# Expert stage of a macaron block: 71 instead of 72 token tiles per call, with one tile in the last pair

## The chip, the cores and the metric

The program runs on one core of one Trainium2 chip. Its engines work side by side, each through its own instruction list, and meet only at semaphores: TensorE (PE, with its weight loads listed apart as PEld), VectorE (DVE), ScalarE (ACT), GpSimd (POOL) and SyncE (SP), which only issues DMA transfers here. The metric is the device time of one execution in microseconds (us); the comparison takes the median of several executions. Smaller is better.

## The reference: what is computed

The input `x` is 4 sequences of 1024 tokens with 128 features, so 4096 tokens. Three layers follow each other:

```
x = x + 0.5 * ffn(layernorm(x))        # call 0 of the expert layer
x = x + mixer(layernorm(x))            # a state-space mixer and its own feed-forward part
x = x + 0.5 * ffn(layernorm(x))        # call 1 of the expert layer, same weights
```

and `ffn` has a shared part and a routed part:

```
shared = (silu(x @ sw1) * (x @ sw2)) @ sw3
w, idx = top_k(softmax(x @ rw + rb), 2)            # 2 of 8 experts for each token
routed = sum over the 2 experts e: w_e * ((silu(x @ ew1[e]) * (x @ ew2[e])) @ ew3[e])
```

Each token meets two of eight experts, so there are 8192 pairs of a token and an expert in each call.

## The kernel before

**Sorting.** For each call POOL scatters 8192 rows of normalised tokens into a DRAM buffer `xs` (L710, 128 rows each). Every expert has a region of its own there. A tile is 128 consecutive rows of one region. The number of tiles that an expert fills is its count divided by 128, rounded up, and DVE works out on the chip where each tile lies (`row_at`) and whose it is (`tile_e`). The program has a fixed number of tiles, `NT = 2 * TOK // P + NE` = 72 for a call. Tiles beyond the filled ones are read from a dummy region, whose rows carry a destination that is out of bounds. The filled tiles can be at most 71: the 8192 rows fill 64 tiles, and rounding up for 8 experts adds less than 8 in all, in whole tiles. How many are filled depends on the data.

**Expert loop.** The tiles go in `NPAIR` = 36 pairs, numbered p. For a pair the work is, in this order:

- SP loads both tiles from `xs` into a ring of 8 slots (L462); `tile_in` counts the landings of each slot.
- PE transposes them (`pe_tiles_t`, L2025), ACT rounds the result to the upper part `xt_hi` (L1018), DVE takes the rest `xt_lo` (L1506) and the destinations `dest` of the rows (L1511).
- PE multiplies with the up weights of the tile's expert, three matmuls of 512 columns for a tile (`pe_up_e`, L2038 to L2040).
- ACT takes the silu (L1026) and DVE the product `hid` (L1521).
- PE transposes `hid` (`pe_hid_t`, L2051, two for a tile), ACT copies it out (L1035), PE multiplies with the down weights (`pe_down_e`, L2064, two for a tile, each of which the trace records as two).
- DVE copies the answer out of PSUM to `y_out`, a ring of 4 slots of two tiles (`dve_answer`, L1531).
- POOL scatters it to the DRAM buffer `ys` with one indirect DMA for each tile (`pool_answers`, L726); `y_stored` counts the landings of each slot. Rows whose destination is out of bounds are skipped.

The order is written out by hand. In step p PE does the up matmuls of pair p + 1, the transposes of `hid` of pair p, the down matmuls of pair p - 1 and the tile transposes of pair p + 3. In the names of the trace, `ps_a` and `ps_b` hold the up products of even and odd pairs, `ps_go` and `ps_tr` the transposes and answers in turn, and `arena` is the memory in which `x_tiles`, `y_out` and the copied `hid` lie.

**End of a call.** SP waits until all four `y_stored` semaphores have their full count (L464), then loads the answers back from `ys` (L469) in blocks of 512 tokens. In call 0 DVE adds them to `x` (L1539), and the mixer starts from that; in call 1 ACT and DVE add them (L1042, L1551, L1555) and SP stores the result (L472).

```
                for r in range(YRING):
                    sp.wait_ge(y_stored[r], 32 * (NPAIR // YRING) * (call + 1))
```

Of the kernel before, what the change touches and what calls it, by code (L numbers as in the profile page):

```python
# [5 lines left out]
F32 = mybir.dt.float32  # L6
# [5 lines left out]
ACT = mybir.ActivationFunctionType  # L12

P = 128
# [74 lines left out]
def macaron(nc, A, out):  # L89
    ctx = ExitStack()  # L90
    with ctx:
# [36 lines left out]
        y_out = part(0, [P, YRING, 2, P])  # L128
# [63 lines left out]

        ps_turn = (ps_k, ps_t, ps_r)

        def ps_tiles(p):
            return ps_turn[(2 * p + 1) % 3][:, 0:2 * P]

        def ps_answers(p):
            return ps_turn[(2 * p + 2) % 3][:, 0:2 * P]

# [209 lines left out]
        def _(sp):  # L410
# [33 lines left out]
            for call in range(2):  # L444

                sp.wait_ge(pads_ready, call + 1)
                pads = table(mybir.EngineType.SP, pad_row, 0, NE, DUMMY - P)
                for e in range(NE):
                    sp.dma_start(xs[bass.ds(pads[e], P), :], fill[:, :]).then_inc(pads_stored, 16)
                sp.wait_ge(tiles_ready, call + 1)  # L450
                at = list(table(mybir.EngineType.SP, row_at, 0, GROUP, DUMMY))
                sp.wait_ge(pads_stored, 16 * NE * (call + 1))
                sp.wait_ge(scattered, 16 * 2 * TOK // P * (call + 1))

                sp.wait_ge(b_ps_ready, 2 * NB * (call + 1))
                for i in range(NT):
                    if i and i % GROUP == 0:
                        at += list(table(mybir.EngineType.SP, row_at, i, min(GROUP, NT - i), DUMMY))
                    if i >= XIN:
                        sp.wait_ge(t_ps_ready, call * NPAIR + (i - XIN) // 2 + 1)  # L460
                        sp.wait_ge(dest_ready, call * NPAIR + (i - XIN) // 2 + 1)
                    sp.dma_start(x_tiles[:, i % XIN, :], xs[bass.ds(at[i], P), :]).then_inc(tile_in[i % XIN], 16)  # L462
                for r in range(YRING):
                    sp.wait_ge(y_stored[r], 32 * (NPAIR // YRING) * (call + 1))  # L464
                ring = BACK[call]
                for n in range(NB):
                    if n >= ring:
                        sp.wait_ge(combined, call * NB + n - ring + 1)
                    sp.dma_start(y_in[call][:, n % ring, :, :], yv[n]).then_inc(block_in[n], 16)  # L469
# [542 lines left out]
        def act_split(act, call, p):  # L1012

            pair = call * NPAIR + p
            act.wait_ge(t_ps_ready, pair + 1)
            if pair >= 2:
                act.wait_ge(up_e_ps_ready, pair - 1)
            act.activation(xt_hi[:, p % 2, :], ps_tiles(p), ACT.Copy).then_inc(hi_ready, 1)  # L1018

        def act_silu_e(act, call, p):  # L1020

            pair = call * NPAIR + p
            act.wait_ge(up_e_ps_ready, pair + 1)
            if pair >= 2:
                act.wait_ge(hid_e_done, pair - 1)
            act.activation(silu_a[:, p % 2, :].rearrange("p (j h) -> p j h", j=2), ps_pair[p % 2][:, :, 0:HID],  # L1026
                           ACT.Silu).then_inc(silu_e_done, 1)

        def act_hid_t(act, call, p):

# [4 lines left out]
            act.activation(hid_t[:, p % 2, :], ps_d, ACT.Copy).then_inc(ht_ready, 1)  # L1035

        def act_finish(act):
            for n in range(NB):
# [463 lines left out]
        def dve_split(dve, call, p):  # L1502

            pair = call * NPAIR + p
            dve.wait_ge(hi_ready, pair + 1)
            dve.tensor_tensor(xt_lo[:, p % 2, :], ps_tiles(p), xt_hi[:, p % 2, :].bitcast(F32),  # L1506
                              ALU.subtract).then_inc(lo_ready, 1)
            for j in range(2):
                i = 2 * p + j
                dve.wait_ge(tile_in[i % XIN], 16 * ((call * NT + i) // XIN + 1))  # L1510
                r = dve.scalar_tensor_tensor(dest[:, i:i + 1], x_tiles[:, i % XIN, P:P + 1], tile_e[:, i:i + 1],  # L1511
                                             x_tiles[:, i % XIN, P + 1:P + 2], ALU.not_equal, ALU.add)
            r.then_inc(dest_ready, 1)

        def dve_hid_e(dve, call, p):

            pair = call * NPAIR + p
            dve.wait_ge(silu_e_done, pair + 1)
            if pair >= 2:
                dve.wait_ge(ht_ps_ready, pair - 1)  # L1520
            dve.tensor_tensor(hid[:, p % 2, 0, :].rearrange("p (j h) -> p j h", j=2),  # L1521
                              silu_a[:, p % 2, :].rearrange("p (j h) -> p j h", j=2), ps_pair[p % 2][:, :, HID:],
                              ALU.mult).then_inc(hid_e_done, 1)

        def dve_answer(dve, call, p):

            pair = call * NPAIR + p
            dve.wait_ge(y_ps_ready, pair + 1)
            if p >= YRING:
                dve.wait_ge(y_stored[p % YRING], 32 * (call * (NPAIR // YRING) + p // YRING))  # L1530
            dve.tensor_copy(y_out[:, p % YRING, :, :], ps_answers(p).rearrange("p (j d) -> p j d", j=2)).then_inc(answer_ready, 1)  # L1531

        def dve_combine(dve, own, call, n):

# [481 lines left out]
        def pe_tiles_t(pe, call, p):  # L2016

            pair = call * NPAIR + p

            if p >= 5:  # L2020
                pe.wait_ge(answer_ready, pair - 4)
            for j in range(2):
                i = 2 * p + j
                pe.wait_ge(tile_in[i % XIN], 16 * ((call * NT + i) // XIN + 1))
                r = pe.transpose(ps_tiles(p)[:, j * P:(j + 1) * P], x_tiles[:, i % XIN, 0:P], ident[:, :])  # L2025
            r.then_inc(t_ps_ready, 1)

        def pe_up_e(pe, call, p, which):

            pair = call * NPAIR + p  # L2030
            pe.wait_ge(lo_ready, pair + 1)
            after(pe, hid_e_done, pair - 1)
            for j in range(2):
                hi = up_hi[:, bass.ds(which[2 * p + j], 1), :].rearrange("p a h -> p (a h)")
                lo = up_lo[:, bass.ds(which[2 * p + j], 1), :].rearrange("p a h -> p (a h)")
                target = ps_pair[p % 2][:, j, :]
                mine = slice(j * P, (j + 1) * P)
                pe.matmul(target, xt_hi[:, p % 2, mine], hi, start=True, stop=False)  # L2038
                pe.matmul(target, xt_hi[:, p % 2, mine], lo, start=False, stop=False)  # L2039
                r = pe.matmul(target, xt_lo[:, p % 2, mine], hi, start=False, stop=True)  # L2040
            r.then_inc(up_e_ps_ready, 1)

        def pe_hid_t(pe, call, p):

            pair = call * NPAIR + p
            pe.wait_ge(hid_e_done, pair + 1)
            after(pe, ht_ready, pair)
            for j in range(2):
                for k in range(2):
                    at = (2 * j + k) * P  # L2050
                    r = pe.transpose(ps_d[:, at:at + P], hid[:, p % 2, 0, at:at + P], ident[:, :])  # L2051
            r.then_inc(ht_ps_ready, 1)

        def pe_down_e(pe, call, p, which):
# [3 lines left out]

            if p + 2 >= NPAIR:
                pe.wait_ge(answer_ready, pair - 2)  # L2060
            for j in range(2):
                for k in range(2):
                    at = (2 * j + k) * P
                    r = pe.matmul(ps_answers(p)[:, j * P:(j + 1) * P], hid_t[:, p % 2, at:at + P],  # L2064
                                  w_down_e[:, bass.ds(which[2 * p + j], 1), k, :].rearrange("p a d -> p (a d)"),
                                  start=(k == 0), stop=(k == 1))
            r.then_inc(y_ps_ready, 1)

# [139 lines left out]
```

## Time and profile before

| | us |
|---|---|
| median of 3 runs | 791.8 (791.72 to 792.77) |
| the profiled execution, its own time | 793.16 |
| span of its trace | 791.1 |
| expert loop of call 0, first to last scatter of answers | 120.9 to 223.9 |
| expert loop of call 1, last scatter of answers | 767.9 |
| PE busy in the span | 649.5 (82%) |
| POOL busy in the span | 519.5 (66%) |

The page gives busy shares of the engines for the whole span, which has five stages: shared feed-forward and routing (0 to 104 us), the experts of call 0 (to 226), the mixer (to about 600, with the routing of call 1 begun inside), the shared part of call 1 (to 652) and the experts of call 1 with the final sum. A share of busy time says little about any one of them. The chain of work that ended last is the view that tells for each stretch which engine set the pace, and the timeline shows the instructions around one place. Idle time is written in square brackets, with what ended it; "issue" there means that the engine waited for nothing that the profile shows.

### The profile page before, as it was taken

What the parts mean: (1) busy time and instruction counts of PE and PEld (TensorE: products, weight loads), DVE (VectorE), ACT (ScalarE), POOL (GpSimd) and SP (SyncE); (2) the same over time, 40 slices, a digit from 0 to 9 for tenths busy, and PEclk for the clock granted to TensorE, in tenths of its full rate; (3) what the DMA queues carried; (4) which work ended last, traced back from release to release, by engine and by line L of the source; (5) the groups of instructions that cost most, each with busy time, mean ns of one, the idle gap of its engine ahead of it and who ended that gap; (6) DMA issues with size and microseconds to landing.
All of it is one profiled execution on the core that took longest, in us unless ns stands there. A gap on an engine that the chain in (4) does not pass through costs nothing.

```text
span 791.1 us, 13711 instructions
## 1 busy us (share of the span) xinstructions
PE 649.5 (82%) x3768; PEld 478.4 (60%) x3768; DVE 548.8 (69%) x1706; ACT 424.9 (54%) x745; POOL 519.5 (66%) x656
## 2 busy tenths in 40 slices
PE   3478979999907298989999997999978979999950
PEld 2245558888802155657576665667635557889840
DVE  5666756656549669897999999899735635566637
ACT  1122224554407999898999998643213214445525
POOL 3777765666646676887898869676754442666660
PEclk9988989999957588999999999979989998999995
DMA  9511223333142000000000000000010113333218
GB/s 264 161 45 51 78 69 85 88 88 92 57 143 77 0 1 1 0 2 1 1 2 1 1 15 15 14 15 22 21 34 25 58 35 87 86 94 89 79 30 316
DMA packets 49368, 46.34 MB, mean 59 GB/s; under 512 B 8456, under 2 KB 42861, under 8 KB 49296
## 3 DMA queue, kind: packets, MB, share of 16 engines
q1 hardware_dynamic: 40592, 28.54, 12.9%
q0 software_dynamic: 8704, 16.93, 6.6%
q8 instruction: 34, 0.56, 0.3%
q14 instruction: 38, 0.31, 0.2%
HBM read 25.30 MB, written 21.19 MB: 59 GB/s over the span
## 4 chain that ended last, share of the span: by engine, by line
PE 30%; POOL 25%; issue 16%; DVE 12%; DMA 8%; ACT 8%; POOLq 1%; SPq 0%; DVEq 0%; ACTq 0%
POOL xs L710 11%; POOL ys L726 11%; DMA xs<-rows,pos 6%; PE ps_tr L1662 4%; PE ps_go L1662 3%; PE ps_tr L2064 2%; PE ps_go L2051 1%; PE ps_go L1833 1%; PE ps_tr L1850 1%; PE ps_go L1837 1%; PE ps_b L1884 1%; POOL rstd L700 1%; PE ps_go L1883 1%; PE ps_a L2038 1%; PE ps_a L2039 1%
## 5 line engine op out<-in xcount | busy, mean ns | idle before, releaser
L726 POOL DMA_INDIRECT ys<-arena,dest x144 | 140.8, 978 | 88.9 <-issue 64.7
L710 POOL DMA_INDIRECT xs<-rows,pos x128 | 127.0, 993 | 76.2 <-DMA xs<-rows,pos 32.3
L1006 ACT ACTIVATE silu_a<-ps_a 128x512 f32<-128x512 f32 x32 | 19.1, 597 | 62.0 <-PE ps_a L2002 62.0
L2064 PE MATMUL ps_tr<-w_down_e,arena 128*128 x384 | 50.7, 275 | 0.0
L1521 DVE TENSOR_TENSOR hid<-silu_a,ps_a 128x512 f32<-128x512 f32 x36 | 24.8, 688 | 34.8 <-ACT silu_a L1026 34.8
L1521 DVE TENSOR_TENSOR hid<-silu_a,ps_b 128x512 f32<-128x512 f32 x36 | 24.8, 688 | 34.3 <-ACT silu_a L1026 34.3
L2064 PEld LDWEIGHTS ps_tr<-w_down_e,arena 128*128 128x128 f32 x384 | 46.7, 192 | 0.0
L1035 ACT ACTIVATE arena<-ps_go 128x512 f32<-128x512 f32 x72 | 42.6, 592 | 2.0 <-PE ps_go L2051 2.0
L1488 DVE TENSOR_TENSOR hid<-silu_a,ps_b 128x512 f32<-128x512 f32 x32 | 21.9, 687 | 31.2 <-PE ps_b L2004 29.3
L2051 PE MATMUL ps_go<-ident,hid 128*128 128x128 f32 x288 | 43.2, 272 | 0.2
L1026 ACT ACTIVATE silu_a<-ps_a 128x512 f32<-128x512 f32 x36 | 21.5, 597 | 38.4 <-PE ps_a L2040 38.4
L1026 ACT ACTIVATE silu_a<-ps_b 128x512 f32<-128x512 f32 x36 | 21.5, 597 | 37.9 <-PE ps_b L2040 37.9
L2051 PEld LDWEIGHTS ps_go<-ident,hid 128*128 128x128 f32 x288 | 35.5, 140 | 10.1 <-DVE hid L1521 0.8
L1018 ACT ACTIVATE xt_hi<-ps_tr 128x256 fp32r<-128x256 f32 x48 | 18.5, 385 | 40.2 <-PE ps_tr L2025 40.2
L1833 PE MATMUL ps_go<-arena,state 128*128 128x128 f32 x128 | 31.7, 332 | 7.8 <-DVE us L1291 6.9
L2012 PEld LDWEIGHTS ps_go<-w_shared_down,hid 128*128 128x128 f32 x256 | 31.2, 194 | 7.7 <-issue 7.7
L1833 PEld LDWEIGHTS ps_go<-arena,state 128*128 128x128 f32 x128 | 21.8, 204 | 19.7 <-issue 13.9
L1963 PE MATMUL ps_tr<-ident,rows 128*128 128x128 f32 x64 | 13.3, 343 | 24.5 <-DVE rows L1404 19.8
L2012 PE MATMUL ps_go<-w_shared_down,hid 128*128 128x128 f32 x256 | 31.5, 276 | 1.7 <-DVE x L1493 1.7
L2038 PE MATMUL ps_a<-up_hi,xt_hi 128*128 x72 | 32.3, 449 | 0.0
L1662 PE MATMUL ps_go<-arena,w_tap 128*128 128x512 f32 x64 | 32.1, 647 | 0.0
L2038 PE MATMUL ps_b<-up_hi,xt_hi 128*128 x72 | 31.8, 441 | 0.0
(368 smaller groups left out, 2042.3 us busy)
## 6 DMA issues: line engine op xcount, KB each, us to landing
arena<-xs SPq DMA_DIRECT2D x144, 65.0 KB, 1.9
rows<-ys SPq DMA_DIRECT2D x8, 512.0 KB, 3.8
arena<-ys SPq DMA_DIRECT2D x8, 512.0 KB, 7.1
ys<-arena,dest POOLq DMA_INDIRECT x144
x<-in_L_attn_x SPq DMA_DIRECT2D x8, 256.0 KB, 4.5
arena<-in_L_ffn_ew SPq DMA_DIRECT2D x4, 512.0 KB, 7.0
xs<-rows,pos POOLq DMA_INDIRECT x128
out<-x SPq DMA_DIRECT2D x8, 256.0 KB, 4.8
```

Source lines behind the costliest of these rows:

```text
L710: pool.indirect_dma_start(xs, bass.IndirectOffsetOnAxis(pos[:, n, i:i + 1], 0), rows[:, n * TT + i % TT, :], None).then_inc(scattered, 16)
L726: pool.indirect_dma_start(ys, bass.IndirectOffsetOnAxis(dest[:, i:i + 1], 0), y_out[:, p % YRING, j, :], None, bounds_check=2 * TOK - 1, o ...
L1026: act.activation(silu_a[:, p % 2, :].rearrange("p (j h) -> p j h", j=2), ps_pair[p % 2][:, :, 0:HID], ACT.Silu).then_inc(silu_e_done, 1)
L1035: act.activation(hid_t[:, p % 2, :], ps_d, ACT.Copy).then_inc(ht_ready, 1)
L1488: dve.tensor_tensor(hid[:, turn % 2, k, :], silu_a[:, k, :], ps_b[:, k, :], ALU.mult).then_inc(hid_done, 1)
L1521: dve.tensor_tensor(hid[:, p % 2, 0, :].rearrange("p (j h) -> p j h", j=2), silu_a[:, p % 2, :].rearrange("p (j h) -> p j h", j=2), ps_pai ...
L1662: r = pe.matmul(target, weights(k), zt[:, shift:shift + BT], start=(k == 0), stop=(k == taps - 1))
L1833: pe.matmul(pb["o"][:, at], state[:, k % 2, p * P:(p + 1) * P], cfs[:, q, k * P:(k + 1) * P], start=True, stop=False)
L2012: r = pe.matmul(ps_d[:, t * P:(t + 1) * P], hid[:, turn % 2, k, t * P:(t + 1) * P], w_shared_down[:, k, :], start=(k == 0), stop=(k == 1))
L2038: pe.matmul(target, xt_hi[:, p % 2, mine], hi, start=True, stop=False)
L2051: r = pe.transpose(ps_d[:, at:at + P], hid[:, p % 2, 0, at:at + P], ident[:, :])
L2064: r = pe.matmul(ps_answers(p)[:, j * P:(j + 1) * P], hid_t[:, p % 2, at:at + P], w_down_e[:, bass.ds(which[2 * p + j], 1), k, :].rearrange ...
```

## The change

The program has `LIVE = NT - 1` = 71 tiles in a call. Pairs 0 to 34 are as they were; pair 35 has one tile. Two helpers say which tiles a pair has and how many landings a ring slot gets in a call:

```diff
+LIVE = NT - 1
+def tiles_of(p):
+    return range(2 * p, min(2 * p + 2, LIVE))
+def in_ring(r, ring, of=1):
+    return sum(i // of % ring == r for i in range(LIVE))
...
-                for i in range(NT):
+                for i in range(LIVE):
...
-                    sp.wait_ge(y_stored[r], 32 * (NPAIR // YRING) * (call + 1))
+                    sp.wait_ge(y_stored[r], 16 * in_ring(r, YRING, 2) * (call + 1))
...
-            for j in range(2):
-                i = 2 * p + j
+            for j, i in enumerate(tiles_of(p)):
                 pool.indirect_dma_start(ys, bass.IndirectOffsetOnAxis(dest[:, i:i + 1], 0),
...
-            act.activation(silu_a[:, p % 2, :].rearrange("p (j h) -> p j h", j=2), ps_pair[p % 2][:, :, 0:HID],
+            act.activation(halves(silu_a[:, p % 2, :], p), ps_pair[p % 2][:, 0:len(tiles_of(p)), 0:HID],
                            ACT.Silu).then_inc(silu_e_done, 1)
...
-            for j in range(2):
-                i = 2 * p + j
-                pe.wait_ge(tile_in[i % XIN], 16 * ((call * NT + i) // XIN + 1))
+            for j, i in enumerate(tiles_of(p)):
+                pe.wait_ge(tile_in[i % XIN], 16 * (call * in_ring(i % XIN, XIN) + i // XIN + 1))
                 r = pe.transpose(ps_tiles(p)[:, j * P:(j + 1) * P], x_tiles[:, i % XIN, 0:P], ident[:, :])
```

The other functions of the loop take the same form: their operand is half as wide for pair 35, and of full width for all others. Slot 7 of the tile ring gets 8 landings in a call and the others 9; slot 3 of the answer ring gets 17 and the others 18.

On PE, at the end of the loop of call 0, this stood before, from the up matmuls of pair 35 (`ps_b`) to the transposes of its `hid`. The first rows are those of its second tile, which come straight behind the three matmuls of its first:

```order
L2038 ISA
L2038 MATMUL ps_b<-up_hi,xt_hi 128x512
L2039 REGISTER_ALU
L2039 MATMUL ps_b<-up_lo,xt_hi 128x512
L2040 MATMUL ps_b<-up_hi,xt_lo 128x512
L2051 MATMUL ps_go<-ident,hid 128x128 x4
L2064 ISA
L2064 MATMUL ps_tr<-w_down_e,arena 128x128
```

and now this stands there, from the matmuls of the first tile on (the lines are numbered 13 higher in the changed kernel here):

```order
L2051 ISA
L2051 MATMUL ps_b<-up_hi,xt_hi 128x512
L2052 REGISTER_ALU
L2052 MATMUL ps_b<-up_lo,xt_hi 128x512
L2053 MATMUL ps_b<-up_hi,xt_lo 128x512
L2064 MATMUL ps_go<-ident,hid 128x128 x4
L2077 ISA
L2077 MATMUL ps_tr<-w_down_e,arena 128x128
```

The block of five rows stands once ahead of the transposes of pair 34 instead of twice, and all that follows on PE moves up by it: the transposes of pair 34, the down matmuls of pair 33, and so on.

On POOL, between the constants of the mixer and its first norm, the scatters of the answers of call 0 stood before in one group of 72 (line 726),

```order
L501 AFFINE_SELECT own_head<-own_head 128x256
L726 DMA ys<-arena,dest 8192x128 x72
L528 TENSOR_SCALAR asmall<-amv 128x4
L529 TENSOR_TENSOR arstd<-asmall,minus_half 128x4
L530 TENSOR_TENSOR asmall<-arstd 128x4
```

and now in one of 71:

```order
L516 AFFINE_SELECT own_head<-own_head 128x256
L740 DMA ys<-arena,dest 8192x128 x71
L543 TENSOR_SCALAR asmall<-amv 128x4
L544 TENSOR_TENSOR arstd<-asmall,minus_half 128x4
L545 TENSOR_TENSOR asmall<-arstd 128x4
```

One scatter is gone at the end of the group, and nothing changes place. The second call has the same two differences, and SP has one load of `xs` fewer in each call.

## Rows read from the trace of the kernel before

**Rows 1.** The page: span, PE and POOL busy, chain by engine.
```profile
span 791.1 us, 13711 instructions
PE 649.5 (82%) x3768; PEld 478.4 (60%) x3768; DVE 548.8 (69%) x1706; ACT 424.9 (54%) x745; POOL 519.5 (66%) x656
...
PE 30%; POOL 25%; issue 16%; DVE 12%; DMA 8%; ACT 8%; POOLq 1%; SPq 0%; DVEq 0%; ACTq 0%
```

**Rows 2.** Timeline of the steady loop: start us, length us, engine, line, operation.
```profile
119.27 0.25 PEld L2025 LDWEIGHTS ps_go<-ident,arena 128*128 128x128 f32 x2
...
122.21 0.25 PEld L2025 LDWEIGHTS ps_tr<-ident,arena 128*128 128x128 f32 x2
...
122.52 0.42 DVE L1531 COPY arena<-ps_tr 128x256 f32<-128x256 f32 x1
...
123.78 0.97 POOL L726 DMA_INDIRECT ys<-arena,dest  x1 [0.54 <-issue]
```

**Rows 3.** Timeline, end of call 0, PE's weight loads and DVE.
```profile
210.28 0.26 PEld L2025 LDWEIGHTS ps_tr<-ident,arena 128*128 128x128 f32 x2
...
210.50 0.19 PEld L2038 LDWEIGHTS ps_a<-up_hi,xt_hi 128*128 128x128 f32 x1
...
213.53 0.42 DVE L1531 COPY arena<-ps_go 128x256 f32<-128x256 f32 x1
...
213.79 0.19 PEld L2038 LDWEIGHTS ps_b<-up_hi,xt_hi 128*128 128x128 f32 x1
...
214.49 0.59 PEld L2051 LDWEIGHTS ps_go<-ident,hid 128*128 128x128 f32 x4
...
216.25 0.42 DVE L1531 COPY arena<-ps_tr 128x256 f32<-128x256 f32 x1
...
218.91 0.42 DVE L1531 COPY arena<-ps_go 128x256 f32<-128x256 f32 x1 [0.61 <-PE ps_go L2064]
```

**Rows 4.** Timeline, end of call 0, POOL's scatters of answers.
```profile
214.79 0.97 POOL L726 DMA_INDIRECT ys<-arena,dest  x1 [0.68 <-issue]
...
217.51 0.97 POOL L726 DMA_INDIRECT ys<-arena,dest  x1 [0.47 <-issue]
...
218.78 0.97 POOL L726 DMA_INDIRECT ys<-arena,dest  x1 [0.30 <-issue]
...
222.61 0.97 POOL L726 DMA_INDIRECT ys<-arena,dest  x1 [0.30 <-issue]
223.89 0.97 POOL L726 DMA_INDIRECT ys<-arena,dest  x1 [0.30 <-issue]
```

**Rows 5.** Chain of work, end of call 0: start us, length us, what.
```profile
223.89 2.10 DMA ys<-arena,dest
...
226.07 3.85 DMA rows<-ys
```

**Rows 6.** DMA from 218 to 226 us: forty slices of 0.2 us, GB/s.
```profile
GB/s 0 0 0 0 0 328 0 0 0 0 0 50 2 0 0 0 0 0 3 0 0 0 0 0 2 1 0 0 0 0 0 3 0 0 0 0 0 3 0 0
```

**Rows 7.** All scatters of answers: shortest, median and longest duration in ns.
```profile
L726 POOL DMA_INDIRECT ys<-arena,dest x144: 969/980/1092, 120.9 to 767.9; - x144
```

**Rows 8.** Timeline, end of call 1, the same engines.
```profile
754.28 0.26 PEld L2025 LDWEIGHTS ps_tr<-ident,arena 128*128 128x128 f32 x2
...
758.79 0.98 POOL L726 DMA_INDIRECT ys<-arena,dest  x1 [0.66 <-issue]
...
762.79 0.98 POOL L726 DMA_INDIRECT ys<-arena,dest  x1 [0.31 <-issue]
...
767.95 0.98 POOL L726 DMA_INDIRECT ys<-arena,dest  x1 [0.30 <-issue]
```

**Rows 9.** Chain of work, end of call 1.
```profile
767.95 2.11 DMA ys<-arena,dest
```

**Rows 10.** Busy us by stretch: PE, PEld, DVE, ACT, POOL, then granted clock, DMA share.
```profile
340.00:350.00 10.00, 9.73 (x37) 5.46 (x36) 8.89 (x16) 9.88 (x15) 9.66 (x11) 0.83 0.01 2
235.00:240.00 5.00, 0.00 (x0) 0.00 (x0) 4.86 (x23) 1.24 (x4) 4.26 (x11) 0.50 0.38 120
```

More of the change, by code:

```diff
@@ L1017, in act_split @@
                 act.wait_ge(up_e_ps_ready, pair - 1)
-            act.activation(xt_hi[:, p % 2, :], ps_tiles(p), ACT.Copy).then_inc(hi_ready, 1)
+            act.activation(xt_hi[:, p % 2, 0:len(tiles_of(p)) * P], ps_tiles(p), ACT.Copy).then_inc(hi_ready, 1)
         def act_silu_e(act, call, p):
@@ L1034, in act_hid_t @@
                 act.wait_ge(y_ps_ready, pair - 1)
-            act.activation(hid_t[:, p % 2, :], ps_d, ACT.Copy).then_inc(ht_ready, 1)
+            width = len(tiles_of(p)) * HID
+            act.activation(hid_t[:, p % 2, 0:width], ps_d[:, 0:width], ACT.Copy).then_inc(ht_ready, 1)
         def act_finish(act):
@@ L1505, in dve_split @@
             dve.wait_ge(hi_ready, pair + 1)
-            dve.tensor_tensor(xt_lo[:, p % 2, :], ps_tiles(p), xt_hi[:, p % 2, :].bitcast(F32),
+            mine = slice(0, len(tiles_of(p)) * P)
+            dve.tensor_tensor(xt_lo[:, p % 2, mine], ps_tiles(p), xt_hi[:, p % 2, mine].bitcast(F32),
                               ALU.subtract).then_inc(lo_ready, 1)
-            for j in range(2):
-                i = 2 * p + j
-                dve.wait_ge(tile_in[i % XIN], 16 * ((call * NT + i) // XIN + 1))
+            for i in tiles_of(p):
+                dve.wait_ge(tile_in[i % XIN], 16 * (call * in_ring(i % XIN, XIN) + i // XIN + 1))
                 r = dve.scalar_tensor_tensor(dest[:, i:i + 1], x_tiles[:, i % XIN, P:P + 1], tile_e[:, i:i + 1],
@@ L1529, in dve_answer @@
             if p >= YRING:
[L1530 to L1531 removed]
+                dve.wait_ge(y_stored[p % YRING], 16 * (call * in_ring(p % YRING, YRING, 2) + 2 * (p // YRING)))
+            dve.tensor_copy(y_out[:, p % YRING, 0:len(tiles_of(p)), :], ps_answers(p).rearrange("p (j d) -> p j d", d=P)).then_inc(answer_ready, 1)
         def dve_combine(dve, own, call, n):
@@ L2032, in pe_up_e @@
             after(pe, hid_e_done, pair - 1)
-            for j in range(2):
-                hi = up_hi[:, bass.ds(which[2 * p + j], 1), :].rearrange("p a h -> p (a h)")
-                lo = up_lo[:, bass.ds(which[2 * p + j], 1), :].rearrange("p a h -> p (a h)")
+            for j, i in enumerate(tiles_of(p)):
+                hi = up_hi[:, bass.ds(which[i], 1), :].rearrange("p a h -> p (a h)")
+                lo = up_lo[:, bass.ds(which[i], 1), :].rearrange("p a h -> p (a h)")
                 target = ps_pair[p % 2][:, j, :]
@@ L2047, in pe_hid_t @@
             after(pe, ht_ready, pair)
-            for j in range(2):
+            for j in range(len(tiles_of(p))):
                 for k in range(2):
@@ L2060, in pe_down_e @@
                 pe.wait_ge(answer_ready, pair - 2)
-            for j in range(2):
+            for j, i in enumerate(tiles_of(p)):
                 for k in range(2):
@@ L2064, in pe_down_e @@
                     r = pe.matmul(ps_answers(p)[:, j * P:(j + 1) * P], hid_t[:, p % 2, at:at + P],
-                                  w_down_e[:, bass.ds(which[2 * p + j], 1), k, :].rearrange("p a d -> p (a d)"),
+                                  w_down_e[:, bass.ds(which[i], 1), k, :].rearrange("p a d -> p (a d)"),
                                   start=(k == 0), stop=(k == 1))
```

11 lines of the change are left out of this document (5 added, 6 removed).

## The prediction

> **What bounds the kernel now.** I read the page first, then the chain of work that ended last, then the timeline at the two places where a call of the experts ends. The page shows no engine that is the bound for the whole span: PE is busy 82% and POOL 66% of it, and the chain gives PE 30% and POOL 25% [rows 1]. So the question is what sets the pace where the removed tile stood, and the tile stood at the very end of each call.
>
> In the steady loop the tile transposes of two neighbouring pairs start at 119.27 and 122.21 us, a period of 2.94 us, and PE has no gap in it. POOL follows: the answer copy starts at 122.52 and the scatter at 123.78, 1.26 us later [rows 2]. Two scatters behind each other take POOL 1.28 us each (below), 2.56 us for a pair, less than 2.94. POOL has room there and PE paces.
>
> At the end this turns round. PE has no more up matmuls to do, and the answer copies come at 213.53, 216.25 and 218.91 us, the last being that of pair 35 [rows 3]. POOL is still issuing: its last scatters start at 218.78, two more in between, then 222.61 and 223.89 [rows 4], (223.89 - 218.78) / 4 = 1.28 us apart. The answer of pair 35 lay ready for over 3 us before its scatter began. What ends the call is the last scatter: the chain goes from its start at 223.89 through 2.10 us of landing to the load of the answers at 226.07 [rows 5], and nothing else runs. Call 1 ends in the same way: 762.79 and 767.95 with three scatters between them, 1.29 us apart [rows 8], and a landing of 2.11 us [rows 9]. Everything behind these two points waits for the loaded answers, the mixer in one case and the final sum in the other.
>
> **What the last scatter carries.** After the peak of 328 GB/s and a remainder of 50 GB/s the DMA moves 3 GB/s or less in any slice [rows 6]. The issues behind it belong to tiles without rows. They cost the same as others: shortest, median and longest scatter are 969, 980 and 1092 ns [rows 7], and the 2.10 us of landing in rows 5 is that of an empty one. So an empty tile is not cheap, and taking it away is worth a whole issue.
>
> **The change part by part.** First the scatter. One issue fewer stands at the end of each queue of POOL: 1.28 us in call 0 and 1.29 us in call 1, all on the path [rows 4, 8].
>
> Second, POOL's unbroken run starts earlier. It begins with the first scatter of pair 32 at 214.79 [rows 4], 1.26 us behind the answer copy of 213.53 [rows 3], so it is tied to PE. Ahead of that answer the change removes one of the two transposes of pair 35's tiles. The two take from 210.28 to 210.50 [rows 3], so one is 0.11 us. In call 1 the same pair of loads stands at 754.28 [rows 8]. The run starts 0.11 us earlier in each.
>
> Third, a small wait inside the run goes. The scatter of pair 33 starts at 217.51, which is 2.72 us and not 2 x 1.28 = 2.56 us behind 214.79 [rows 4], because its answer copy of 216.25 was late [rows 3]. In the new order three up matmuls of pair 35 are missing ahead of the down matmuls of pair 33. They take from 213.79 to 214.49 [rows 3], 0.70 us. With the transpose the answer is ready 0.81 us earlier if PE paces it, at 215.44, and its scatter could start at 216.70. POOL is free for it at 214.68 + 2.56 = 217.24. So POOL paces from there, with 0.5 us to spare, and the 0.16 us are gained. DVE does the product of pair 35 ahead of this copy; it is half as wide and its silu starts earlier too, so it does not hold the copy up.
>
> The sum for call 0: seven scatters stand from pair 32 on, with six steps between them, so the last starts at 214.68 + 6 x 1.28 = 222.36 in place of 223.89, a gain of 1.53 us. For call 1: 758.79 - 0.11 + 6 x 1.29 = 766.42 in place of 767.95 [rows 8], again 1.53 us. Together 3.06 us.
>
> The rest costs and gives nothing. The other down matmuls and transposes of pair 35, its shorter copies on ACT and DVE and one load on SP all lie before the answer copy of 218.91, over 3 us ahead of need. If that cover were gone, the 0.5 us above would be the first to be felt. The first 35 pairs have operands of the same shape, the semaphores have other constants, and no wait is added. SP waits for the same four semaphores, and the fullest still comes last. PE's list is shorter by nine rows in each call. What this does to the fetching of instructions no row shows; I bound it by -0.3 and +0.3 us, the size of POOL's ordinary gap between scatters [rows 4], and take zero.
>
> Against the profiled execution this makes the span 791.1 - 3.06 = 788.0 us. Its own time, 793.16, lies 1.4 us above the median of 791.8. A shift in two places applies to each run alike, so I take it off the median: 791.8 - 3.1 = 788.7 us.
>
> **A rule against it.** Each scatter keeps POOL for 1.28 us though its data are nil [rows 4, 6]. The Trainium skill, "DMA: Bandwidth & Descriptors", section "Anatomy of one DMA — SWDGE (gpsimd) path", says that nearly all of the fixed 2 us of such a transfer is the receipt of the write at its end, and that making the descriptors is small. By that rule issues would overlap with landings and one issue fewer would be worth near nothing, which is the time of rival (a). The landing of 2.10 us agrees [rows 5]; the steps between issues do not, and the sum goes by the steps.
>
> **Rivals.** (a) The end is not set by the last issue but by the last scatter with data. Then the empty issue was free, and only the earlier start counts: 0.11 + 0.16 = 0.27 us a call, 791.3 us. For it speaks that all data had gone by 220.4 us, 1.6 us behind the issue of 218.78 [rows 4, 6]. Against it speaks the chain, in which the load of the answers follows the landing of the issue at 223.89 by 0.08 us [rows 5], as it must if each semaphore counts every scatter.
>
> (b) The gain of call 0 is given back in the mixer, through TensorE's clock. The clock is at half, 1.2 GHz, when the mixer begins (0.50 at 235 to 240 us, PE idle before), and inside it there are drops such as 340 to 350 us with a granted mean of 0.83 while PE is busy 9.73 of 10 us [rows 10]. That mean is (1 - 0.83) / 0.5 = a third of the stretch, 3.4 us, at half speed, and at worst half of that, 1.7 us, is lost. All that follows stands 1.5 us earlier, and a drop may come in or go. One more makes 788.7 + 1.7 = 790.4 us, within 0.2% of before; one fewer makes 787.0. The Trainium skill, "TensorE: Matmul & The Clock Gate", section "Part 1: The HAM clock gate", says that the gate watches activity on a count that runs free of the kernel, so that the same program ramps at different places from run to run. By that, such drops would be spread over runs of both kernels alike, and the sum would stay. The three runs of before lie within 1.05 us of each other.
>
> (c) Slower: the same mechanism several times. Two more drops (3.4 us) eat the gain and decide the sign, and three make 788.7 + 5.1 = 793.8 us. For it: the mixer keeps PE, ACT and POOL all over 9 us of 10 busy in rows 10, so that lost PE time has little slack. Against it: nothing inside the mixer changes its order, and PE is idle for as long as before ahead of it, since its own end and the load of the answers both move up by about 1.5 us.
>
> (d) The change doesn't take the issue away because the list of POOL is the same. The order shows 71 in place of 72, so I give this no chance.
>
> **How the numbers follow.** Forecast, the whole 3.1 us: 0.80, with a spread of about 0.9 us from the bounds and from medians of three runs. One more drop of the clock: 0.08. One fewer: 0.04. Empty scatter free (a): 0.05. Slower (c): 0.03. What a measurement can tell from no change is 0.2%, 1.6 us. Faster by more than that are the forecast and one drop fewer, 0.84. Within it lie (a) and one more drop, 0.13. Slower is 0.03. The range reaches from 787.4 to 790.3 us: it holds the forecast's own spread and most of the case with one more drop, and leaves out 787.0 and (a).
>
> **What would show it.** After the change POOL's list of answers should have 142 scatters. In call 0 the run of steps of 1.28 us should begin with the first scatter of pair 32, 0.1 us earlier than 214.79, with no step of 1.45 us in it, and the last should start at 222.4; in call 1 the load of the answers should follow the last scatter by 2.2 us as now, and the rest, 21 us, should keep its length. The mixer's stretch should be as long as before: from the load of the answers of call 0 to the last scatter of call 1, 767.95 - 226.07 = 541.9 us, it should be 1.5 us shorter, 540.4. I am wrong if the last scatter starts less than 1 us earlier, which would mean that PE or a landing paces the end, or if that stretch grows, which would be the clock.

## The result and the profile after

| | before | changed kernel |
|---|---|---|
| median of 8 runs each, us | 792.52 (791.64 to 793.4) | 789.51 (788.24 to 791.18) |
| ratio, 95% interval | 1 | 0.9963 (0.9949 to 0.9976) |
| span of the trace, us | 791.1 | 789.0 |

The kernel became 3.0 us faster where 3.1 was forecast; the interval of the ratio reaches from 1.9 to 4.0 us. The page of the changed kernel is nearly that of before [rows 1]: two scatters fewer, shares the same.

```profile
span 789.0 us, 13649 instructions
PE 643.9 (82%) x3748; PEld 473.3 (60%) x3748; DVE 545.4 (69%) x1704; ACT 423.9 (54%) x745; POOL 519.5 (66%) x654
...
PE 46%; POOL 15%; DVE 12%; issue 10%; DMA 8%; ACT 8%; SPq 0%; POOLq 0%; DVEq 0%; ACTq 0%
```

The last line, the chain by engine, gives PE 46% and POOL 15%, where it was 30% and 25%. That is no change of the loop. The chain is followed back from the end: in the kernel before it stays with POOL through the last pairs, and in the changed kernel it leaves POOL at the scatter of 217.92, goes to a copy of DVE, and follows PE from there. The shares of a chain can jump like this where two engines run at one pace.

The timeline of the end of call 0 shows the unbroken run that was forecast, as [rows 3, 4] did for the kernel before (columns: start us, length us, engine, line, operation).

```profile
210.97 0.14 PEld L2038 LDWEIGHTS ps_tr<-ident,arena 128*128 128x128 f32 x1
...
214.10 0.42 DVE L1545 COPY arena<-ps_go 128x256 f32<-128x256 f32 x1
...
215.36 0.97 POOL L740 DMA_INDIRECT ys<-arena,dest  x1 [0.57 <-issue]
...
216.14 0.42 DVE L1545 COPY arena<-ps_tr 128x256 f32<-128x256 f32 x1 [0.49 <-PE ps_tr L2077]
...
216.64 0.97 POOL L740 DMA_INDIRECT ys<-arena,dest  x1 [0.30 <-DVE arena L1545]
...
217.92 0.97 POOL L740 DMA_INDIRECT ys<-arena,dest  x1 [0.30 <-DVE arena L1545]
219.20 0.97 POOL L740 DMA_INDIRECT ys<-arena,dest  x1 [0.30 <-issue]
...
223.03 0.97 POOL L740 DMA_INDIRECT ys<-arena,dest  x1 [0.30 <-issue]
```

One tile is transposed where it was two. The answer copy of pair 32 starts at 214.10, its first scatter 1.26 us later, and from there seven scatters stand 1.28 us apart up to 223.03, with no longer step among them. The two small gains can be read one by one. From the last tile transpose to this answer copy it is 214.10 - 210.97 = 3.13 us where it was 213.53 - 210.28 = 3.25 [rows 3]. From the first scatter of pair 32 to that of pair 33 it is 217.92 - 215.36 = 2.56 us where it was 2.72 [rows 4]. The chain of this stretch again goes from the last scatter through its landing to the load of the answers:

```profile
223.03 2.09 DMA ys<-arena,dest
...
225.21 3.73 DMA rows<-ys
```

All scatters of answers together (count, shortest, median and longest duration in ns, first and last start):

```profile
L740 POOL DMA_INDIRECT ys<-arena,dest x142: 970/982/1092, 121.6 to 765.8; - x142
```

The gain is best read from the length of POOL's queue, from the first to the last scatter of a call, since what happens ahead of the loop shifts both ends:

| | call 0 | call 1 |
|---|---|---|
| before | 120.87 to 223.89, 103.02 | 664.86 to 767.95, 103.09 |
| changed | 121.56 to 223.03, 101.47 | 664.24 to 765.79, 101.55 |
| shorter by | 1.55 | 1.54 |

That is 3.09 us, and 3.06 were forecast. The two spans differ by only 2.1 us because in these two executions the first scatter of the changed kernel came 0.69 us later and the stretch between the calls took 0.24 us more (441.21 against 440.97), both outside of the two loops. The prediction named one more length as a sign, from the load of the answers of call 0 to the last scatter of call 1. It is 765.79 - 225.21 = 540.6 us, against 541.9 before and 540.4 forecast.

### The profile page after: what moved, and what is told of

It reads as the page before. It is cut to its first block, busy times and chain, and to the rows that moved or that the text cites. A ratio compares the mean times of both kernels' runs of the same rounds, so it can differ in the third digit from the quotient of the medians.

```text
span 789.0 us, 13649 instructions
## 1 busy us (share of the span) xinstructions
PE 643.9 (82%) x3748; PEld 473.3 (60%) x3748; DVE 545.4 (69%) x1704; ACT 423.9 (54%) x745; POOL 519.5 (66%) x654
## 4 chain that ended last, share of the span: by engine, by line
PE 46%; POOL 15%; DVE 12%; issue 10%; DMA 8%; ACT 8%; SPq 0%; POOLq 0%; DVEq 0%; ACTq 0%
POOL xs L725 11%; DMA xs<-rows,pos 6%; PE ps_tr L2077 5%; PE ps_go L2064 4%; PE ps_tr L1676 4%; PE ps_go L1676 3%; PE ps_go L2077 2%; PE ps_a L2051 2%; PE ps_a L2053 2%; PE ps_a L2052 2%; PE ps_b L2053 2%; PE ps_b L2051 2%; PE ps_b L2052 2%; PE ps_go L1847 1%; PE ps_tr L1864 1%
## 5 line engine op out<-in xcount | busy, mean ns | idle before, releaser
L740 POOL DMA_INDIRECT ys<-arena,dest x142 | 139.1, 980 | 88.3 <-issue 62.4
L1536 DVE TENSOR_TENSOR hid<-silu_a,ps_a 128x512 f32<-128x512 f32 x36 | 24.8, 688 | 35.7 <-ACT silu_a L1040 35.7
L1536 DVE TENSOR_TENSOR hid<-silu_a,ps_b 128x512 f32<-128x512 f32 (+1 forms) x36 | 24.2, 673 | 32.9 <-ACT silu_a L1040 31.6
L1503 DVE TENSOR_TENSOR hid<-silu_a,ps_b 128x512 f32<-128x512 f32 x32 | 21.9, 686 | 30.9 <-PE ps_b L2018 29.0
L1040 ACT ACTIVATE silu_a<-ps_b 128x512 f32<-128x512 f32 (+1 forms) x36 | 21.1, 585 | 37.0 <-PE ps_b L2053 37.0
L1032 ACT ACTIVATE xt_hi<-ps_tr 128x256 fp32r<-128x256 f32 (+1 forms) x48 | 18.3, 380 | 41.5 <-PE ps_tr L2038 41.5
L1522 DVE TENSOR_TENSOR xt_lo<-ps_tr,xt_hi 128x256 fp32r<-128x256 f32 (+1 forms) x48 | 20.1, 419 | 16.7 <-ACT xt_hi L1032 16.4
```

The costliest lines, as they stand in the source:

```text
L1040: act.activation(halves(silu_a[:, p % 2, :], p), ps_pair[p % 2][:, 0:len(tiles_of(p)), 0:HID], ACT.Silu).then_inc(silu_e_done, 1)
L1536: dve.tensor_tensor(halves(hid[:, p % 2, 0, :], p), halves(silu_a[:, p % 2, :], p), ps_pair[p % 2][:, 0:len(tiles_of(p)), HID:], ALU.mult) ...
```

## The experiments

The runs were made in three groups, each with its own runs of the kernel before on its chip. "Length" is from first to last scatter of a call.

### Only the scatter is left out

The kernel before, with the 72nd scatter of each call not issued:

```diff
+                if i == NT - 1:
+                    continue
                 pool.indirect_dma_start(ys, bass.IndirectOffsetOnAxis(dest[:, i:i + 1], 0),
```

(and 17 for 18 scatters in the counts of ring slot 3).

> The kernel before, without the scatter of tile 71 and with nothing else changed: PE, ACT and DVE still do the whole pair 35. The tile holds no rows with these inputs. Theory (POOL's issues pace the end of a call, an empty one costs as much as a full one): the stretch from the first to the last scatter of answers, 103.02 us in call 0 and 103.09 in call 1 of the kernel before, gets 1.28 us shorter in each call, to 101.74 and 101.80, and the time falls by 2.6 us, a ratio of 0.9968. The end of the queue keeps its step of 1.44 us ahead of the scatter of pair 33. Rival (the end is set by the last scatter with data, an empty issue is free): the load of the answers starts as long behind the scatter of tile 67 as before, ratio 1.000.

Measured: ratio 0.9980 (0.9966 to 0.9995). Lengths 101.74 and 101.80 us, 1.28 and 1.29 below before. The end of its timeline has the old step ahead of pair 33's scatter, 217.77 - 216.32 = 1.45 us, and then steps of 1.28:

```profile
215.04 0.97 POOL L728 DMA_INDIRECT ys<-arena,dest  x1 [0.69 <-issue]
216.32 0.97 POOL L728 DMA_INDIRECT ys<-arena,dest  x1 [0.30 <-issue]
217.77 0.97 POOL L728 DMA_INDIRECT ys<-arena,dest  x1 [0.47 <-issue]
219.04 0.97 POOL L728 DMA_INDIRECT ys<-arena,dest  x1 [0.30 <-issue]
...
222.87 0.97 POOL L728 DMA_INDIRECT ys<-arena,dest  x1 [0.30 <-issue]
225.03 1.28 SPq L469 DMA_DIRECT2D rows<-ys  x3
```

An empty issue costs its whole step. The rival by which only scatters with rows count falls; the load of the answers comes 2.16 us behind the last issue here, and 2.18 in the kernel before.

### Half a pair on PE, all 72 scatters

The changed kernel, with a scatter to out-of-bounds places (`nowhere`) at the end of each call:

```diff
+            if p == NPAIR - 1:
+                pool.wait_ge(route_const, ROUTE_CONST)
+                pool.indirect_dma_start(ys, bass.IndirectOffsetOnAxis(nowhere[:, 0:1], 0),
+                                        y_out[:, p % YRING, 1, :], None, bounds_check=2 * TOK - 1,
+                                        oob_is_err=False).then_inc(y_stored[p % YRING], 16)
```

> The changed kernel, with a 72nd scatter of answers put back at the end of each call, all of whose destinations are out of bounds. PE, ACT and DVE do one tile in pair 35. Theory: only the earlier start of POOL's run and the step of 1.44 us are gained, 0.27 us a call: the stretch from first to last scatter is 102.75 and 102.82 us, the time 0.5 us below the kernel before, ratio 0.9993, and the steps at the end are all 1.28 us. Rival (PE's work of the removed tile is what the end waited for, half a pair of 2.94 us): the whole 1.5 us a call is there without the missing issue, ratio 0.996.

Measured: lengths 102.74 and 102.81 us, as the theory has them, and the unbroken run of steps:

```profile
213.59 0.97 POOL L742 DMA_INDIRECT ys<-arena,dest  x1 [0.58 <-issue]
...
222.53 0.97 POOL L748 DMA_INDIRECT ys<-arena,nowhere  x1 [0.30 <-issue]
```

From 213.59 to 222.53 are seven steps of 1.277. So of 1.55 us for each call 1.28 belong to the issue and 0.27 to the shorter work ahead of it, on PE, ACT and DVE together. But the whole kernel was slower than that says: ratio 1.0033 (1.0014 to 1.0052) where 0.9993 was expected. The lengths are as short as expected, so the 3 us lie outside of them. The trace of this run (span 790.8 us) does not have them; one of the same kernel in the third group does, and this is taken up below.

### One scatter more, at the end or in the loop

The same piece in the kernel before, once behind the last pair and once behind pair 16 (`if p == 16`).

> The kernel before, with one more scatter without rows behind the last of each call, so 73. Theory: each issue at the end costs its own step, so 104.30 and 104.37 us from first to last scatter and 2.6 us more time, ratio 1.0032. Rival (an empty issue is free): ratio 1.000.

> The kernel before, with one more scatter without rows in the middle of the loop of each call, behind pair 16, so 73 as in the other run. Theory (PE paces the loop with 2.94 us a pair, POOL needs 2.56 and has 0.38 us to spare): the 1.28 us are made up within four pairs, the stretch from first to last scatter stays 103.0 and 103.1 us, ratio 1.000. Rival (POOL paces the whole loop, its idle time being overhead of its waits): the issue costs 1.28 us in each call here too, ratio 1.0032.

Measured: at the end 1.0023 (1.0009 to 1.0038), lengths 104.32 and 104.41 us, each 1.3 us more. In the loop 0.9992 (0.9976 to 1.0009), lengths 103.02 and 103.06 us, as without it. The timeline of POOL around the added scatter shows how the loop takes it in:

```profile
168.61 0.97 POOL L728 DMA_INDIRECT ys<-arena,dest  x1 [0.30 <-issue]
169.88 0.97 POOL L734 DMA_INDIRECT ys<-arena,nowhere  x1 [0.30 <-issue]
171.16 0.97 POOL L728 DMA_INDIRECT ys<-arena,dest  x1 [0.30 <-issue]
172.44 0.97 POOL L728 DMA_INDIRECT ys<-arena,dest  x1 [0.30 <-DVE arena L1540]
...
177.54 0.97 POOL L728 DMA_INDIRECT ys<-arena,dest  x1 [0.30 <-issue]
179.07 0.97 POOL L728 DMA_INDIRECT ys<-arena,dest  x1 [0.56 <-issue]
```

The idle time of 0.7 us that stands ahead of every pair elsewhere shrinks to POOL's own gap of 0.30 for three pairs; at 179.07 it is 0.56 already, so that POOL has nearly caught up. The same instruction is free in the loop and costs 1.3 us at its end. The label "issue" on idle time doesn't tell these apart; the steps do.

### Another form, 70 tiles, and an order with earlier answers, on a disturbed chip

The second group ran on a chip on which the kernel before took 847.64 us. The changed kernel's chain of waits shows why:

```profile
208.81 2.16 another core or an unknown queue
210.97 0.02 issue
210.99 0.61 ACT arena L1050
```

Engines stood for 2 to 3 us again and again, and for what ended these waits the profile names no engine and no queue of this core. The call of the experts took 121 us there instead of 101. Its times tell little of a change of 3 us, which shows in their intervals.

> The changed kernel again, unchanged, for the comparison within this group. Theory: ratio 0.9961, from first to last scatter 101.5 us in both calls. Rival (half of the gain is lost to the clock in the mixer on average): 0.998.

> The changed kernel again with 72 scatters of answers, in another way: SP still loads tile 71 and DVE still makes its destinations, all out of bounds, and POOL scatters with them; no constant of out-of-bounds places is added. PE's and ACT's work and DVE's other work on tile 71 are left out. Theory (POOL's issues pace the end): from first to last scatter 102.75 and 102.82 us, as in the first form of this run, and the time 0.5 us below the kernel before, ratio 0.9993. If the 2 us above that, which the first form had outside the two loops, belong to one issue more behind a PE that ends sooner (the mixer starts after a longer rest of PE), this form has them too, ratio 1.002 to 1.003; if they belong to how that program lay or to its runs, they are gone.

> The changed kernel with 70 tiles, 35 whole pairs, and pair 35 left out; with these inputs 68 and 67 tiles hold rows in the two calls. Theory: against the kernel before, a whole pair of the PE-paced loop goes and the end stays as it was, with its step of 1.44 us: 2.94 us a call, from first to last scatter 100.08 and 100.15 us, time 5.9 us lower, ratio 0.9926. Rival (POOL's issues pace all of the loop): two issues, 2.56 us a call, 100.46 us from first to last, ratio 0.9935; (the clock gives part back): the two stretches as in the theory, but a ratio nearer to 1.

Measured against the kernel before on that chip: the changed kernel 0.9955 (0.9918 to 0.9993); the form with 72 scatters and `dest` of tile 71 kept 0.9997 (0.9970 to 1.0024); 70 tiles 0.9953 (0.9922 to 0.9985), an interval that takes in both expected values and 71 tiles as well. The lengths there were 121.16, 122.16 and 118.39 us in call 0, with standstills of 2 to 3 us in all, so that neither the second form nor the price of a whole pair was settled.

The fourth kernel of the group changes PE's order; `between` issues the down matmuls of pair p - 1, and DVE copies the answer first, to match:

```diff
+                if j == 1 or p == NPAIR - 1:
+                    between()
                 pe.matmul(target, xt_hi[:, p % 2, mine], hi, start=True, stop=False)
```

> The changed kernel with another order on PE: in each step the down matmuls of pair p - 1 stand between the two tiles of the up matmuls of pair p + 1 and no longer behind the transposes of pair p; DVE copies the answer ahead of the product of pair p + 1. Theory (what ends a call is POOL's run of seven issues, and this run starts when the answer of pair 32 is there): that answer comes 0.70 + 0.44 = 1.14 us earlier, measured from the last tile transpose of a call to its last scatter 10.9 us in place of 12.06, and the time falls 2.3 us below the changed kernel, ratio 0.993 to the kernel before, if PE keeps its 2.94 us a pair. Rival (PE has to wait for ACT's copy of hid, 0.75 us behind its transposes, with 0.92 us between them): each wait that shows up is paid 36 times in a call, and even 0.1 us of it makes the kernel 7 us slower.

Measured: 0.9914 (0.9880 to 0.9949) on the disturbed chip, the lowest ratio of all, and yet its trace had a period of 3.12 us in quiet stretches. Its two lengths in that trace, 116.87 and 122.91 us, lie on either side of the changed kernel's 121.16 and 120.39. So it ran again in the third group, on a chip without these standstills.

> The kernel with the down matmuls between the two tiles of the up matmuls in all steps, once more. In its first trace PE's period was 3.12 us where nothing else disturbed it, because the down matmuls wait for ACT's copy of hid. Theory: 0.18 us for each of some 35 pairs in two calls are 12.6 us, less 2.3 for the earlier end, so 10 us slower than the changed kernel, ratio 1.009 to the kernel before, wherever the engines are not held up by other things. Rival (the order is as fast as its first ratio of 0.991 says): 0.991.

Measured: 1.0123 (1.0097 to 1.0149), above the 1.009 that was expected, lengths 108.74 and 108.70 us. The timeline of PE and of ACT's copy, one period:

```profile
150.19 0.38 PE L2038 MATMUL ps_tr<-ident,arena 128*128 128x128 f32 x2
...
150.45 0.59 ACT L1050 ACTIVATE arena<-ps_go 128x512 f32<-128x512 f32 x1
...
150.88 0.40 PE L2055 MATMUL ps_b<-up_hi,xt_lo 128*128 x1
151.18 1.15 PE L2079 MATMUL ps_go<-w_down_e,arena 128*128 x8
152.09 0.48 PE L2053 MATMUL ps_b<-up_hi,xt_hi 128*128 x1
...
152.41 0.39 PE L2054 MATMUL ps_b<-up_lo,xt_hi 128*128 x1
...
153.31 0.38 PE L2038 MATMUL ps_tr<-ident,arena 128*128 128x128 f32 x2
```

The period is 153.31 - 150.19 = 3.12 us, 0.18 more than 2.94. The wait for ACT's copy is only part of it. The down matmuls start at 151.18, which is 0.14 us behind the end of that copy (150.45 + 0.59) and 0.30 behind the last up matmul of the first tile, where the step between up matmuls is 0.23: 0.07 us. The up matmuls are also begun twice in a period, and behind the first of a block 0.32 us pass (152.09 to 152.41) in place of 0.23: 0.09 us more. Why the first takes longer no run shows. Over 35 pairs this makes 6.3 us a call, and the lengths grew by 7.2. The earlier answers don't pay for it: from the last tile transpose to the last scatter it is 12.60 us, where 10.9 was expected at first and the changed kernel has 12.06, because the answers of the last pairs come late here and POOL waits 0.97 and 1.04 us for two of them. One kernel, two chips, and opposite signs: on the disturbed chip a wait of 0.18 us a pair drowns among standstills of 2 us, and why the order was faster there was not tried.

### A gentler order

The changed kernel with the down matmuls of pair p - 1 ahead of the transposes of pair p, and between the two tiles only for the answer of pair 32:

```diff
                     pe_up_e(pe, call, p + 1, which,
+                            (lambda: pe_down_e(pe, call, p - 1, which)) if p == NPAIR - 3 else None)
+                if p >= 1 and p != NPAIR - 3:
+                    pe_down_e(pe, call, p - 1, which)
                 if 0 <= p < NPAIR:
                     pe_hid_t(pe, call, p)
-                if p >= 1:
-                    pe_down_e(pe, call, p - 1, which)
```

> The changed kernel with the down matmuls of pair p - 1 ahead of the transposes of pair p in each step, and only in the step of pair 32's answer (p = 33) between the two tiles of the up matmuls; DVE copies the answer ahead of the product of pair p + 1. Theory: the copy of hid by ACT has more time than before in all steps but one, so PE keeps 2.94 us a pair; the answer of pair 32 comes 0.44 + 0.70 us earlier, of which POOL, still at pair 31, can use 0.44 + 0.38. From the last tile transpose to the last scatter 11.2 in place of 12.06 us, time 1.6 us below the changed kernel, ratio 0.994 to the kernel before. Rival (PE waits in the new order as in the run with the answers in between): a period over 2.94 us, 0.1 us of it makes 7 us, ratio over 1.003.

Measured: 0.9979 (0.9961 to 0.9997). The period in the loop stays 2.95 us, so that rival falls. From the last tile transpose (210.84) to the last scatter (222.59) are 11.75 us, against 12.06 in the changed kernel: 0.31 us gained of 0.82. Most of the rest, 0.40 us, went into one late answer:

```profile
214.99 1.00 PEld L2079 LDWEIGHTS ps_tr<-w_down_e,arena 128*128 128x128 f32 x8 [0.55 <-issue]
...
215.80 0.97 POOL L740 DMA_INDIRECT ys<-arena,dest  x1 [0.30 <-issue]
216.22 0.42 DVE L1545 COPY arena<-ps_tr 128x256 f32<-128x256 f32 x1 [1.13 <-PE ps_tr L2079]
...
217.48 0.97 POOL L740 DMA_INDIRECT ys<-arena,dest  x1 [0.71 <-issue]
```

With a short last pair only three up matmuls stand between the transposes of pair 33 and its down matmuls, too few to cover ACT's copy; PE waits 0.55 us, the answer comes at 216.22 and POOL's step is 1.68 us. In the changed kernel this answer had 0.5 us to spare, and the new order spent them. It is 3 us below the changed kernel's median in the same group, but mostly for the reason of the next part, so no gain over it is shown beyond the 0.3 us for each call in the trace. The ratio of 0.994 that was expected lies outside of the interval.

### The third group, and what the clock does to the whole

> The changed kernel, unchanged, as the measure for this group. Theory: ratio 0.9961 to the kernel before, 101.5 us from first to last scatter in both calls, 12.06 us from the last tile transpose of call 0 to its last scatter.

> The changed kernel with a 72nd scatter without rows at the end of each call, once more, in its first form. Theory: from first to last scatter 102.75 and 102.81 us as before, and a time 2.6 us above the changed kernel, ratio 0.9993 to the kernel before. Rival (this program is slowed outside the loops by 2 to 3 us, by more half-speed stretches of TensorE): ratio 1.003 again, with a granted clock near 0.908 in most of its runs where the others have 0.916.

Measured: the changed kernel 0.9997 (0.9976 to 1.0018); the form with a 72nd scatter 1.0034 (1.0011 to 1.0057). The lengths are once more 101.46 and 101.54 us, and 102.74 and 102.83 us. So the gain of 3.1 us in the two loops was there in both traces of the changed kernel on an undisturbed chip, and in this group it was lost again elsewhere.

The times show how. Of the 12 runs of the changed kernel five took 789.4 to 790.2 us, with a mean granted clock of 0.917 to 0.922, and seven 794.0 to 795.7 us, six of these at 0.903 to 0.909. A median between two such clusters jumps with one run: it is 794.50 us against 793.26 for the kernel before, while the means are 792.9 and 793.2.

Cutting each trace at its scatters of answers shows where the time lies (us):

| trace | mean granted clock | call 0 | between the calls | call 1 |
|---|---|---|---|---|
| before | 0.916 | 103.02 | 440.97 | 103.09 |
| changed, first comparison | 0.915 | 101.47 | 441.21 | 101.55 |
| 72nd scatter kept, first time | 0.917 | 102.74 | 442.30 | 102.81 |
| changed, third group | 0.903 | 101.46 | 447.03 | 101.54 |
| 72nd scatter kept, third group | 0.909 | 102.74 | 446.12 | 102.83 |

Between the calls stand the mixer and the routing and shared part of call 1. The largest difference is at one place in the mixer. Busy us by stretch (PE, PEld, DVE, ACT, POOL, then granted clock and DMA share), of the changed kernel's execution in this group first, of its first execution below, and of the kernel before last:

```profile
300.00:500.00 200.00, 191.86 (x1048) 127.40 (x1049) 178.42 (x427) 179.42 (x286) 161.92 (x218) 0.92 0.01 4
...
520.00:530.00 10.00, 8.27 (x60) 6.48 (x59) 9.62 (x39) 4.55 (x8) 8.16 (x9) 0.83 0.07 22
530.00:540.00 10.00, 10.00 (x38) 6.14 (x38) 9.07 (x22) 4.35 (x8) 4.14 (x4) 0.65 0.06 20
```

```profile
300.00:500.00 200.00, 191.54 (x1073) 128.38 (x1074) 180.77 (x435) 182.68 (x292) 164.26 (x218) 0.95 0.01 4
530.00:540.00 10.00, 9.67 (x61) 7.59 (x61) 9.69 (x31) 6.33 (x11) 6.33 (x7) 1.00 0.06 20
```

```profile
530.00:540.00 10.00, 10.00 (x40) 6.29 (x40) 9.11 (x24) 5.50 (x8) 5.02 (x5) 0.73 0.04 13
```

PE is busy for 10.00 and 9.67 of the ten microseconds, and does 38 matmuls in one and 61 in the other. The two executions are not at quite the same work there, but the granted clock goes with the difference: (1 - 0.65) / 0.5 = 70% of the stretch was at 1.2 GHz, and with 0.83 in the ten microseconds ahead of it the drop lasted 7.0 + 3.4 = 10.4 us. In the mixer the work comes in blocks, each of which ends with an add to `x` on DVE. The fifth and the sixth of these adds, in the same order of executions:

```profile
528.85 0.69 DVE L1339 TENSOR_TENSOR x<-x,ps_tr 128x512 f32<-128x512 f32 x1
...
559.14 0.68 DVE L1339 TENSOR_TENSOR x<-x,ps_tr 128x512 f32<-128x512 f32 x1
```

```profile
525.62 0.69 DVE L1339 TENSOR_TENSOR x<-x,ps_tr 128x512 f32<-128x512 f32 x1
...
552.48 0.68 DVE L1339 TENSOR_TENSOR x<-x,ps_tr 128x512 f32<-128x512 f32 x1
```

```profile
527.34 0.69 DVE L1324 TENSOR_TENSOR x<-x,ps_tr 128x512 f32<-128x512 f32 x1
...
557.52 0.68 DVE L1324 TENSOR_TENSOR x<-x,ps_tr 128x512 f32<-128x512 f32 x1
```

These are 30.29, 26.86 and 30.18 us. So this drop cost 3.4 us of the 5.8 by which the long execution is longer between the calls; 2.4 more stand ahead of the first add. But the drop alone does not make an execution long. The trace of the kernel before has it as well and is short: it needed 2.2 us less from the eighth add to the first scatter of call 1 (78.58 against 80.75 in the changed kernel's first trace). Nor does the length from the first to the second add tell them apart: it is 35.7 us in all four traces of the third group, long and short, and 34.3 in all six of the others.

How often an execution falls low differs between the programs. Counting runs with a mean granted clock under 0.912 on the undisturbed chips, a bound that was chosen with the runs in view:

| PE's last pair | kernels | runs under 0.912 |
|---|---|---|
| whole | before (two groups), scatter left out, scatter added at the end or in the loop | 4 of 100 |
| half | changed kernel (first comparison and third group), 72nd scatter kept (two groups), both new orders | 24 of 62 |

The programs within the second row are not alike: changed kernel 0 of 8 in the first comparison and 6 of 12 in the third group, 72nd scatter kept 7 of 12 twice, the gentler order 4 of 12, the earlier answers 0 of 6. On the disturbed chip the two kinds do not differ: 26 of 42 with a whole last pair (the kernel before and 70 tiles), 20 of 31 with half a pair.

So on the undisturbed chips half a pair on PE goes together with a lower granted clock, and the missing scatter does not: the kernel that only leaves out the scatter has 0 of 12. What joins the two is open, and that the clock is the cause of the longer time is read from the traces; no run set it. It isn't the length of PE's rest ahead of the mixer, at least not alone: that is 21.68 us before and 21.76 in both traces of the changed kernel, the short and the long one. The half-pair programs are also shorter by nine rows on PE in each call, so that everything in the mixer lies at other places in its instruction list; no run separated this from the work itself.

## Why the prediction was right, and where it fell short

**What ends a call.** Right. The last issue of POOL does, empty or not; leaving out only that one took 1.28 and 1.29 us off each queue, adding one put 1.3 on.

**The scatter, the earlier start, the step of 1.44 us.** 1.28, 0.11 and 0.16 us a call were forecast. In the traces they are 1.28, 0.12 and 0.16. The two last together, 0.27 in the forecast, were 103.02 - 102.74 = 0.28 us with all scatters kept. The answer copies agree: from 214.10 to 216.14 are 2.04 us, and the forecast had 215.44 - 213.42 = 2.02.

**The rule against it.** The Trainium skill, "DMA: Bandwidth & Descriptors", section "Anatomy of one DMA — SWDGE (gpsimd) path", puts the fixed cost at about 2.0 us, most of it the receipt of the write, and calls the making of descriptors small. The sum agrees: 2.09 to 2.10 us from the start of an issue to its landing. The split does not show here, since POOL itself is busy for 0.97 us of them, and what decided is that the next issue starts 1.28 us behind the last.

**The median.** 3.1 us forecast, 3.0 measured in the deciding comparison; 789.51 us is inside the range and 0.8 above the 788.7 of the sum. Here the result flatters the forecast. In the third group the same kernel was 794.50 us, outside of my range of 787.4 to 790.3, with the mechanism of rival (b): stretches of half clock more in the mixer. I gave it 0.08 and took one drop of 1.7 us as its size, and I argued from the three runs of before that it would be spread over both kernels alike. The runs contradict this step: 6 of 20 executions of the changed kernel had the low clock and 2 of 64 of the kernel before. One drop cost 3.4 us and not 1.7, because it lasted some 10 us and not 3.4, and an affected execution of the changed kernel was some 5 us longer. So the price of rival (b) was half of what one drop measured, and its chance was too small. That the deciding comparison had none of the long executions, 0 of 8 where the third group had 6 of 12, is luck as far as the runs tell. The range had a flaw of its own: it was said to hold most of the case with one more drop, whose 790.4 us lies above its upper end of 790.3. The Trainium skill, "TensorE: Matmul & The Clock Gate", section "Part 1: The HAM clock gate", says that the gate's count runs free of the kernel. That would fit two kinds of execution of one program, but not that two programs have them in such unequal shares.

**The sign that was named for it.** The stretch from the load of the answers of call 0 to the last scatter of call 1 was to tell of the clock if it grew. It did its work: 540.6 us in the first trace of the changed kernel, and 770.06 - 223.65 = 546.4 in the one of the third group.

**Slower.** Rival (c) didn't happen for the changed kernel: 0.9997 in its worst group, though its median there was 1.2 us above that of the kernel before. The form with 72 scatters and half a pair shows how near it was: 1.0033 and 1.0034.

## What to carry to other kernels

At the end of a pipelined loop ask which queue is still running when the others are done: there an instruction costs its full step, even with no data behind it, while the same instruction inside the loop may be free. Read such an edge from the steps between the issues and from a length with both ends in the same stretch, not from the median alone; a gain of 0.4% can be the same to 0.02 us in two traces and still come and go in the total with a stage that the edit does not touch. And don't take a ratio from a disturbed chip as a verdict: the order that looked best there at 0.991 was 1.012 elsewhere.

## What the hardware showed that was not expected

- A scatter all of whose rows are out of bounds keeps POOL for 0.97 us and its queue for 1.28 (1.29 in call 1), as a full one does, and lands after 2.1 us.
- The kernel before took 792 to 793 us in three comparisons and 848 us in a fourth, on another chip, with standstills of engines of 2 to 3 us for which the profile names no engine or queue of the core.
- Executions of the changed kernel on one chip fell into two clusters 5 us apart, 789.4 to 790.2 and 794.0 to 795.7 us, with mean granted clocks of 0.917 to 0.922 and, in six of seven, 0.903 to 0.909. Programs with half a pair of matmuls less at the end of a loop were under 0.912 in 24 of 62 runs and the others in 4 of 100; a disturbed chip showed no such difference.
